# Small early loads in three packs, ids first on ACT's queue, and another order of stages on all engines

## The reference

```python
h = concat([patches @ W.T + b, table[x_txt] + pe], axis=1)           # (16, 548, 64)
h = h + attn(layernorm(h))    # LN, q/k/v, relu(q k^T * scale) v, residual, relu FFN 64-128-64, LN
h = h + moe1(layernorm(h))    # top-1 of 8 experts with a capacity, relu, 64-256-64
h = h + attn2(layernorm(h))   # 16 heads of 4: k, v layernormed, q (k^T v) / 548, proj, exact gelu, residual
h = h + moe2(layernorm(h))    # top-2 of 8 experts, LN gain per expert, exact gelu, 64-256-64
```

## Time and profile before

| | us |
|---|---|
| device time, median of 3 runs (lowest, highest) | 793.96 (793.09, 794.42) |
| the profiled execution: its own time / span of its trace | 796.31 / 794.2 |
| PE busy, share of the span, instructions | 710.0, 89%, 4619 |
| PEld busy | 481.1, 61% |
| DVE busy | 615.5, 77%, 2308 |
| ACT busy | 452.0, 57%, 956 |
| POOL busy | 436.3, 55%, 470 |

### The profile page before, as it was taken

One profiled execution on the slowest core, in us unless ns is written; L12 is line 12 of the kernel. 1 busy time (PEld: TensorE's weight loads), 2 busy tenths in 40 slices (PEclk: granted clock), 3 DMA queues, 4 the chain that ended last, 5 costly groups with the idle time before them and its releaser, 6 DMA issues. The chain is left out here.

```text
span 794.2 us, 15813 instructions
## 1 busy us (share of the span) xinstructions
PE 710.0 (89%) x4619; PEld 481.1 (61%) x4619; DVE 615.5 (77%) x2308; ACT 452.0 (57%) x956; POOL 436.3 (55%) x470
## 2 busy tenths in 40 slices
PE   3699999998997799995689999999999999999994
PEld 1477776676764457663346666666666666666672
DVE  4568989999889546577789998999999899775421
ACT  2266656565552056660356776666777666677552
POOL 4654327776566700236757877777787774323321
PEclk9599999999999799996599999999999999999998
DMA  7930000000000013321032122333321222333020
GB/s 215 331 120 14 11 12 19 20 22 11 4 5 4 5 40 88 96 76 25 7 63 61 35 44 57 66 66 67 66 54 24 64 60 65 66 66 65 14 60 14
DMA packets 60976, 43.69 MB, mean 55 GB/s; under 512 B 29100, under 2 KB 56252, under 8 KB 60636
## 3 DMA queue, kind: packets, MB, share of 16 engines
q1 hardware_dynamic: 51820, 36.35, 18.3%
q0 software_dynamic: 7200, 4.17, 2.6%
q10 hardware_dynamic: 1872, 2.18, 0.9%
HBM read 31.66 MB, written 13.47 MB: 57 GB/s over the span
## 5 line engine op out<-in xcount | busy, mean ns | idle before, releaser
L787 ACT ACTIVATE scratch<-psum,fb 128x512 f32<-128x512 f32 (+2 forms) x288 | 171.9, 666 | 55.4 <-PE psum L1213 41.5
L700 PE MATMUL psum<-scratch,w_fw 128*64 128x256 f32 (+2 forms) x1152 | 136.5, 376 | 1.6 <-DVE prob L1050 0.8
L569 POOL DMA_INDIRECT uu<-expert_out,slot_i x80 | 85.7, 1071 | 89.8 <-DMA expert_out<-X 69.4
L610 POOL TENSOR_TENSOR prob<-prob,scratch 128x256 f32<-128x256 f32 (+2 forms) x126 | 80.8, 642 | 94.2 <-DVE scratch L1050 91.0
L1151 POOL DMA_INDIRECT slots_buf<-xt,slot_i x80 | 81.5, 1018 | 50.5 <-issue 32.5
L700 PEld LDWEIGHTS psum<-scratch,w_fw 128*64 128x64 f32 x1152 | 78.6, 136 | 41.6 <-issue 11.4
L1137 POOL DMA_INDIRECT emb<-in_table,w_ids x64 | 63.3, 989 | 58.7 <-DVE stats L1579 36.0
L1212 PE MATMUL psum<-kh,fw_hi 128*128 128x512 f32 x176 | 77.4, 440 | 3.7 <-ACT scratch L787 3.7
L1477 ACT ACTIVATE prob<-psum 128x292 f32<-128x292 f32 (+1 forms) x160 | 55.2, 397 | 40.8 <-PE psum L1279 40.5
L1050 DVE SCALAR_TENSOR_TENSOR scratch<-psum,w_fb,X 128x256 f32<-128x256 f32 (+1 forms) x119 | 53.8, 459 | 25.6 <-PE psum L700 25.1
L1213 PE MATMUL psum<-kh,fw_lo 128*128 128x512 f32 x176 | 69.5, 395 | 0.0
(11 more groups left out here) (272 smaller groups left out, 1642.3 us busy)
## 6 DMA issues: line engine op xcount, KB each, us to landing
X<-share_buf SPq DMA_DIRECT2D x32, 512.0 KB
slots_buf<-zeros SPq DMA_DIRECT2D x8, 352.0 KB, 5.4
expert_out<-zeros SPq DMA_DIRECT2D x8, 352.0 KB, 4.3
out<-H SPq DMA_DIRECT2D x16, 128.0 KB
X<-in_patches ACTq DMA_DIRECT2D x3, 576.0 KB, 8.0
slots_buf<-xt,slot_i POOLq DMA_INDIRECT x80, 2.2
uu<-expert_out,slot_i POOLq DMA_INDIRECT x80, 2.5
emb<-in_table,w_ids POOLq DMA_INDIRECT x64, 2.5
```

The lines of the kernel that those rows point to most:

```text
L569: pool.indirect_dma_start(yg[b % 2][0:rows, s, :], None, expert_out, bass.IndirectOffsetOnAxis(slot_i[0:rows, b, (s + 1) % SLOTS:(s + 1) % ...
L610: pool.tensor_tensor(total[t % 2][:, 0:z], total[t % 2][:, 0:z], part[m % PARTS][:, 0:z], ALU.add).then_inc(sem("summed"), 1)
L700: last = pe.matmul(bank(6 + n % 2)[h * D:(h + 1) * D, 0:z], w["fw2"][:, e * J + j, :], hid[(J * n + j) % (J * UNITS)][:, h * z:(h + 1) * z ...
L787: act.activation(hid[m % (J * UNITS)][:, 0:z], bank(2 + m % 4)[:, 0:z], ACT.Gelu, bias=fb1[:, e * J + j:e * J + j + 1]).then_inc(sem("gelu ...
```

## The change

**Loads.** The host joins 23 small tensors into three arrays, each padded to 128 rows: pack_first (385 columns, 197 KB), pack_attn (708 columns, 362 KB) and pack_ffn (738 columns, 378 KB). In the kernel the old names become views into the packs. SP now issues tok_w, pack_attn, pack_first; ACT issues ids, the patches, pack_ffn; POOL issues no load of ids. Each reader waits for the pack that it needs.

```diff
+PACKS = dict(
+    pack_first=dict(ident=(P, P), tok_b=(P, 1), pe=(P, TXT, D)),
+    pack_attn=dict(norm_b=(D, 1), norm_g=(P, 1), wq=(P, 4 * D), wk=(P, 4 * D), wv=(P, 2 * D), bq=(P, 1), bk=(P, 1), bv=(P, D)),
+    pack_ffn=dict(w1=(P, 2 * F_ATTN), b1=(P, 1), w2=(P, D), b2=(P, 1), fg=(P, D), fb=(P, D), gw=(P, 2 * E), gb=(P, E),
+                  tri=(P, P), order=(P, GMAX * SLOTS, E), base=(P, E), limit=(P, E)),
+)
...
         @block.sync
         def _(sp):
-            for n in ("ident", "tok_b"):
-                sp.dma_start(w[n][:], i[n]).then_inc(sem("patches_in"), 16)
-            for n in EARLY[:EARLY_BY_SP]:
-                sp.dma_start(w[n][:], i[n]).then_inc(sem("early_in"), 16)
-            sp.wait_ge(sem("patches_in"), 48)
+            sp.dma_start(w["tok_w"][:], i["tok_w"]).then_inc(sem("tok_w_in"), 16)
+            for n in ("pack_attn", "pack_first"):
+                sp.dma_start(w[n][:], i[n]).then_inc(sem(n), 16)
             for q in range(PATCH_LOADS):
                 sp.wait_ge(sem(f"patches_in{q}"), 16)
-            sp.wait_ge(sem("early_in"), EARLY_IN)
+            for n in PACKS:
+                sp.wait_ge(sem(n), 16)
...
         @block.gpsimd
         def _(pool):
-            pool.dma_start(w["ids"][:], i["ids"]).then_inc(sem("ids_in"), 16)
             pool.wait_ge(sem("ids_in"), 16)
...
                 if b == 0:
-                    pool.wait_ge(sem("prep"), 1)
+                    pool.wait_ge(sem("pack_ffn"), 16)
                 pool.wait_ge(sem("norm1b"), (b + 1) * PER["norm1b"])
...
         @block.tensor
         def _(pe):
...
-            pe.wait_ge(sem("patches_in"), 48)
+            pe.wait_ge(sem("pack_attn"), 16)
+            pe.matmul(bank(7)[:, 0:1], w["wq"][0:D, 0:P], w["norm_b"][:], start=True, stop=True)
+            pe.matmul(bank(7)[:, 1:2], w["wk"][0:D, 0:P], w["norm_b"][:], start=True, stop=True)
+            pe.matmul(bank(7)[:, 64:64 + D], w["norm_b"][:].to_broadcast([D, P]), w["wv"][0:D, 0:D], start=True, stop=True).then_inc(sem("bias_prod"), 1)
+            pe.wait_ge(sem("tok_w_in"), 16)
             for k in range(KC):
...
+            pe.wait_ge(sem("pack_first"), 16)
             for h in range(2):
                 pe.wait_ge(sem("img_t"), h + 1)
...
-            pe.wait_ge(sem("early_in"), EARLY_IN)
-            pe.matmul(bank(7)[:, 0:1], w["wq"][0:D, 0:P], w["norm_b"][:], start=True, stop=True)
...
             pe.wait_ge(sem("prep"), 1)
...
             def ffn1(b):
+                if b == 0:
+                    pe.wait_ge(sem("pack_ffn"), 16)
...
         @block.scalar
         def _(act):
-            act.dma_start(w["tok_w"][:], i["tok_w"]).then_inc(sem("patches_in"), 16)
+            act.dma_start(w["ids"][:], i["ids"]).then_inc(sem("ids_in"), 16)
...
-            for n in EARLY[EARLY_BY_SP:]:
-                act.dma_start(w[n][:], i[n]).then_inc(sem("early_in"), 16)
+            act.dma_start(w["pack_ffn"][:], i["pack_ffn"]).then_inc(sem("pack_ffn"), 16)
...
-            act.wait_ge(sem("patches_in"), 48)
+            act.wait_ge(sem("pack_first"), 16)
...
-        def norm_stats(dve, st, src, mv):
+        def norm_stats(dve, st, src, mv, image=None, images=0):
             for s in range(SLOTS):
+                if s == IMG and image is not None:
+                    dve.wait_ge(image, images)
                 st(dve.bn_stats(stats[:, s, :], src[:, s, :]))
...
-            dve.wait_ge(sem("early_in"), EARLY_IN)
-            dve.wait_ge(sem("img_h"), 1)
-            def prep(_):
+            def tables(_):
+                dve.wait_ge(sem("pack_ffn"), 16)
                 step_of(dve.tensor_copy(tri_b[:], w["tri"][:]))
                 step_of(dve.tensor_copy(carry[:], w["base"][:]))
+                sync()
+            def prep(_):
+                dve.wait_ge(sem("pack_attn"), 16)
                 dve.wait_ge(sem("bias_prod"), 1)
...
             def norm1a(b):
-                if b == 8:
-                    dve.wait_ge(sem("img_h"), 2)
+                if b == 0:
+                    dve.wait_ge(sem("pack_first"), 16)
...
-                norm_stats(dve, st, H[:, b], mv1[b % 2])
+                norm_stats(dve, st, H[:, b], mv1[b % 2], sem("img_h") if b % 8 == 0 else None, b // 8 + 1)
```

A few lines of the tables:

```diff
-        DVE_ONCE = ((39.1, "prep", 0), (176.25, "late_weights", 0), (715.75, "moe_gains", 0), (762.5, "low_moe", 0))
-        POOL_ONE = ((8.25, "gather_a"), (38.75, "gather_b"), (124.5, "offset"), (364.75, "scatter_a"), (384, "scatter_b"))
+        DVE_ONCE = ((10, "prep", 0), (60, "tables", 0), (176.25, "late_weights", 0), (715.75, "moe_gains", 0), (762.5, "low_moe", 0))
+        POOL_ONE = ((7.5, "gather_a"), (28.5, "gather_b"), (135.5, "offset"), (352, "scatter_a"), (364.75, "scatter_b"))
...
+        POOL_MOVED = {("gather_a", 2): -22, ("gather_a", 6): -7, ("gather_a", 7): -36, ("gather_a", 8): -6, ("gather_a", 11): -22,
...
+                     ("roots4", 3): -2, ("roots4", 4): -4, ("roots4", 7): -2.4, ("roots4", 8): -1, ("roots4", 12): -16, ("roots4", 15): -2.4,
+                     ("roots5", 12): -1, ("roots5", 13): -2.3, ("roots_kv", 2): -6, ("roots_kv", 9): -2, ("roots_kv", 12): -2, ("square", 6): -2,
...
+                     ("place", 11): -17, ("place", 15): -14, ("q_low", 0): -36, ("q_low", 2): -5, ("q_low", 5): -3, ("q_low", 9): -3,
```

More of the change, by code:

```diff
@@ L1 @@
+import math
 from contextlib import ExitStack
@@ L173, in early_fusion_kernel @@
                 w[name] = sb("w_" + name, list(i[name].shape), i[name].dtype)
+        for pack, parts in PACKS.items():
+            at = 0
+            for name, shape in parts.items():
+                cols = math.prod(shape[1:])
+                w[name] = w[pack][0:shape[0], at:at + cols]
+                if len(shape) == 3:
+                    w[name] = w[name].rearrange("p (a c) -> p a c", a=shape[1])
+                at += cols
         ident = w["ident"]
@@ L261, in early_fusion_kernel @@
                    "root3"), (271, "stack3"))
-        DVE_ONE = ((30.75, "norm1a"), (46.75, "norm1b"), (104.5, "q_low"), (112.25, "k_low"), (126.75, "vals"), (168, "resid"), (212.25, "norm2a"),
-                   (226.25, "norm2b"), (235, "norm3a"), (249.25, "norm3b"), (268.5, "gate"), (286.75, "place"))
+        DVE_ONE = ((30.75, "norm1a"), (44.5, "norm1b"), (104.5, "q_low"), (112.25, "k_low"), (126.75, "vals"), (168, "resid"), (212.25, "norm2a"),
+                   (226.25, "norm2b"), (235, "norm3a"), (244.25, "norm3b"), (268.5, "gate"), (286.75, "place"))
@@ L271, in early_fusion_kernel @@
[L271 to L274, removed]
-                      ("offset", 10): -28, ("offset", 11): -52, ("offset", 12): -67, ("offset", 15): 154, ("scale", 0): -13, ("scatter_b", 0): -9,
-                      ("scatter_b", 1): -7, ("scatter_b", 5): -11, ("scatter_b", 6): -11, ("summed", 0): -4, ("summed", 8): -2, ("summed", 67): -3,
-                      ("summed", 87): -3, ("summed", 104): -2}
@@ L407, in early_fusion_kernel @@
         block = ctx.enter_context(nc.Block())
-        EARLY = [n for n in ("pe", "norm_b", "norm_g", "wq", "wk", "wv", "bq", "bk", "bv", "w1", "b1", "w2", "b2", "fg", "fb", "gw", "gb", "tri", "order", "base", "limit")]
         MIDDLE = ["fln_b", "fln_g", "fb1", "wkv", "kv_b", "ak", "vg", "vb", "diag", "heads"]
-        LATE = [n for n in w if n not in EARLY + MIDDLE + ["ids", "tok_w", "tok_b", "ident"]]
-        EARLY_BY_SP = 12
-        EARLY_IN, MIDDLE_IN, LATE_IN = 16 * len(EARLY), 16 * (len(MIDDLE) + 1), 16 * (len(LATE) + 1)
+        PACKED = [n for parts in PACKS.values() for n in parts]
@@ L414, in early_fusion_kernel @@
+        LATE = [n for n in w if n not in MIDDLE + PACKED + list(PACKS) + ["ids", "tok_w"]]
+        MIDDLE_IN, LATE_IN = 16 * (len(MIDDLE) + 1), 16 * (len(LATE) + 1)
         B_STEPS = [(e, c, t) for c, t in ((0, 3), (3, 2), (5, 4), (9, 2)) for e in range(E)]
@@ L1829, in _ @@
             table = dict(resid=resid, q_low=q_low, norm1a=norm1a, norm2a=norm2a, gate=gate, norm3b=norm3b, k_low=k_low, vals=vals, norm1b=norm1b, norm2b=norm2b,
-                         place=place, norm3a=norm3a, prep=prep, late_weights=late_weights, moe_gains=moe_gains, low_moe=low_moe)
+                         place=place, norm3a=norm3a, prep=prep, tables=tables, late_weights=late_weights, moe_gains=moe_gains, low_moe=low_moe)
             for name, b in in_order(DVE_ONE, DVE_MOVED, DVE_ONCE):
@@ L1928, in host_inputs @@
     )
+    for pack, parts in PACKS.items():
+        cols = []
+        for name, shape in parts.items():
+            flat = np.asarray(h.pop(name), np.float32).reshape(shape[0], -1)
+            cols.append(np.concatenate([flat, np.zeros((P - shape[0], flat.shape[1]), np.float32)]))
+        h[pack] = np.concatenate(cols, 1)
     return {n: np.ascontiguousarray(v) for n, v in h.items()}
```

211 lines of the change are left out of this document (110 added, 101 removed), and 79 rows, old and new, of tables (ACT_MOVED, DVE_MOVED, PE_MOVED).

## The result

The changed kernel takes 806.94 us (median of four runs, 802.08 to 808.19) beside 794.19 of the kernel before on the same chip: a ratio of 1.0137, 95% interval 1.0102 to 1.0171. (The ratio compares the means; the two medians lie 12.8 us apart.) A second timing against it (the last experiment) gave 1.0113 [1.0080, 1.0146]. So it is slower by 9 to 11 us, where 6.2 us less had been forecast; the time lies outside the range of 777.5 to 798.5.

A forecast was written before the change was run, and what follows sets the result against it. PE was taken as the limit in the long stretches, with DVE close behind. Terms -4.5 (ramp), -3.5 (order), +0.5 (mixed) and +1.3 (table loads) sum to -6.2, from 793.96 to 787.8 us; own range 783 to 791.5, overall 777.5 to 798.5.

The forecast's parts named there:

- ids and the first gather: At the start, ids at the head of ACT's queue land in 2.5 us; first gather at 3.4 instead of 8.88.
- The image: In norm1a(0), the image wait moves to the fifth statistic; aggregates end at 14.7 instead of 17.47, t1 at 17.2.
- the part on packs: Start of PE: the bias products' wait for pack_attn hides behind the patch load, with some 3 us to spare.
- The ramp: Up to the first scores, earlier loads and part one's new order give a lead of 4.5 us, bounds 2 and 6.
- Passing 286: Before the first expert's transposes, PE's own chain ends last by some 3 us, so the start's lead passes.
- Table loads: ACT's second part: 40 table loads instead of 34, 7.7 us more of ACT, of which +1.3 shows; bounds 0 and 7.7.
- C: Rival, chance 0.18: ACT's six added table loads come on PE's path, +7.7, and the order's gain is gone: 797.7.
- D: Rival, chance 0.04: a stop behind each added table load as long as the load, 15.4 us in all: 805.4.
- The rest of the new order -3.5; bounds -12 and +4: In the two long stretches, the new order removes an eighth of PE's 29.8 us idle.
- mixed(1) ahead of kv_b(0), +0.5: In the hole from 350 to 400 us, this new order on DVE costs 0.5 us, bounds 0 and 3.
- The holds on DVE: low_w keeps its place behind offset(13), so the hold stretching a DVE add to 5.97 us beside it stays.
- The prediction's own test: PE's idle from 400 to 750 us: well under 14 us says rival A, above 20 that the order lost.

The follow-up runs named there:

- the last experiment: The changed kernel, unchanged, timed again against the kernel before: 804.40 us, ratio 1.0113.
- the other half: Loads and part one of the kernel before, with the changed order on PE, ACT and DVE from the experts on, against the kernel before: 804.53 us, 1.0109.
- the old order in the window 290 to 430: Changed kernel with old experts' order and, for part-two table times 290 to 430, old order on PE, DVE and ACT, against the kernel before: 796.47 us, 0.9995.

## Why the prediction was wrong, by its steps

- **ids and the first gather:** right. 3.41 us, forecast 3.4.
- **The image:** right in kind, with the wait at the fifth statistic; the aggregates end at 15.70 where 14.7 was forecast, and t1, at 18.01 instead of 17.2, is late by nearly as much. The image came a little later than the value taken, within its bounds. The wait for pack_attn did not hide with 3 us to spare, as the part on packs had it: the bias products could start only at 6.92, when the pack was in (some 4.7 had been worked out), so the first patch product starts at 8.36 in place of 7.62.
- **The ramp:** -4.0 where -4.5 was forecast, and the clock is full from 32 us instead of 39. But the reason was partly wrong: the loads alone give -4.4, the new order of part one nothing measurable on top. And the agreement is in part luck: the traced execution of the kernel before took 796.31 us, 2.1 more than the median, and the other half, with the same start, reaches the first scores 1.9 us before it.
- **Passing 286:** right. The first expert transposes start at 280.57 (forecast near 281). With the old order behind them the lead reaches the end, but for the 3.3 us that the loads alone lose at half speed near 404 us. In the time it is worth 0.0026 to 0.0042, 2 to 3.3 us, less than the 4.5 counted.
- **Table loads:** the count is right. Lines of ACT in the changed kernel, which answer to the earlier trace rows (busy us, mean ns, idle time before):

```profile
L818 ACT ACT_TABLE_LOAD x18 | 23.1, 1283 | 0.3
L767 ACT ACT_TABLE_LOAD x11 | 14.1, 1283 | 0.2
L762 ACT ACT_TABLE_LOAD x6 | 7.7, 1283 | 0.1
L773 ACT ACT_TABLE_LOAD x3 | 3.8, 1283 | 0.1
L792 ACT ACT_TABLE_LOAD x2 | 2.6, 1283 | 0.0
```

  They are 40, at 1.283 us each. 34 loads were no faster than 40; whether the term was +1.3 or 0 these intervals can't tell. Rivals C and D did not happen: C's 7.7 us are excluded, and D's 805.4 is near the measured time by luck. The Trainium skill, page ScalarE: Activation LUTs, section What ACT_TABLE_LOAD costs, puts a switch at about 2.66 us with its drain; the rows show 1.283 us and 0.7 us of idle time ahead of all 40, and no run here shows the drain.
- **"The rest of the new order -3.5; bounds -12 and +4":** this is the step that failed. By the ratios (changed less loads alone, 0.0155 to 0.0179) it cost 12 to 14 us. Going back to the old order of the experts gave some 3 to 5 us by the ratios (in the traces more: the 2.2 to 2.9 lost up to t4(2), and the 3.3 to 3.5 at half speed near 407 us, which is gone there too), and the old order in the window 290 to 430 some 6.7 more; what is left is 2.9 us (0.9995 less 0.9958), and these two intervals still overlap, by 0.0006. The step took the idle time as something that a new order lowers, and bounded the other side by a third of the waits for gelu; but the waits that grew were those for DVE, which was busy 302.05 of 350 us. That this left it too little slack for a stage put a little late is argued, not shown. And the sum had no term for the clock, whose half-speed stretch near 407 us goes with 3.3 to 3.5 us.
- **mixed(1) ahead of kv_b(0), +0.5:** not seen. With the old experts' order in front of it the lead at t4(2) is that at b_turn(0), within 0.3 us.
- **The holds on DVE:** the prediction left them as they were, and they hardly fell. An instruction of DVE beside low_w, another one than before, still takes 6.00 us beside 4.57, as in the earlier trace rows:

```profile
183.49 6.00 DVE L1781 TENSOR_TENSOR zt<-zt,rs 128x320 f32<-128x320 f32 x1
...
184.56 4.57 POOL L1198 TENSOR_TENSOR ew_lo<-scratch,ew_hi 128x2048 fp32r<-128x2048 f32 x1
```

  Summed over all DVE instructions stretched beyond the median of their kind, worked out from both traces: 37.0 us in 89 before, 33.7 in 81 after. 3.3 us less on DVE did not shorten its chain where PE waits for it.

The prediction's own test had it right: "above 20 says that the order lost", and PE's idle time from 400 to 750 is 23.1 us.

What stays open: which stage in the window, and which unit among the experts, makes the chain late; and why half-speed stretches come at other places in two executions of the same kernel. Lists swapped on one engine alone are slower still, and moving gram only moved the wait. Why DVE's chain is late there, with the same work and a little less of holds, was not traced to one instruction.

Two versions beat both kernels: the loads alone (0.9958), and the changed loads and part one with the old order behind (0.9963 and 0.9974).

## What to carry to other kernels

An early gain of a few us at the start is kept to the end, or most of it, if the order behind it stays as it is: take the loads and leave the rest. A new order of stages on a kernel whose PE and DVE are as busy as here (95% and 86% from 400 to 750 us) should be priced with a loss as large as the largest gain hoped for (here 12 us), and with the half-speed stretches that may come with PE's new idle time. Where PE's wait names a producer, take the wait away and look whether the idle time falls; if it turns up at the next stage, the cause is further up.

## What the runs showed of the hardware

- Half-speed stretches inside a stage that ran at full speed before: 13.65 us behind 13 us in which PE worked 9.02, and 6.83 us behind a wait of 1.74. Four more fill stages ahead of the first took it away, and 6.83 us came back at 450. The traces with a stretch of 10 to 14 us near 407 lose 3.3 to 3.5 us there, those that keep the full clock nothing.
- A wait of that length is not enough by itself: the kernel before has one of 1.7 us for kvnorm at the full clock (its longest among the waits above), and the changed kernel's second trace has the same wait of gram(8), 1.73 us, with no fall behind it. Where the half speed falls differs between two executions of one kernel.
- A small load ahead of the large ones: ids, issued first on ACT's queue at 0.73 us and ahead of the patches, landed in 2.4 us and let the first gather start at 3.41, where the same load, the first on POOL's own queue but issued at 1.27 us, took 7.3. No run separates the queue from the time of issue and from the smaller number of other loads.

```profile
w_ids<-in_ids ACTq DMA_DIRECT2D x1, 32.0 KB, 2.4
```
